# Four graph networks on one core: in the plain nodes' stream, the second and third layer's work moved one turn back

## The reference

```python
# network 0, four attention layers; a node always has itself as a neighbour
h = x @ W
alpha = leaky_relu((h @ a_s)[src] + (h @ a_d)[dst] + (ea @ We) @ a_e)
out = segment_sum(h[src] * segment_softmax(alpha, dst)[:, None], dst) + b
x = layernorm(out) * g + beta
# network 1: relations, three cells; messages relu(h[src] + relvec[rel])
# network 2: three layers
h = relu(h @ Ws0.T + mean_of_neighbours(h) @ Wn0.T + b0); prev = h
h = relu(h @ Ws1.T + mean_of_neighbours(h) @ Wn1.T + b1 + prev)
h = h @ Ws2.T + mean_of_neighbours(h) @ Wn2.T + b2
# network 3: products along edges, then a last layer norm
```

## Time and profile before

| what | value |
|---|---|
| time, median of 3 runs | 5097.33 us (5092.68 to 5098.29) |
| profiled execution | 5105.29 us, its span 5103.5 us |
| PE busy over the span | 3761.0 us, 74% |
| DVE busy | 3758.0 us, 74% |
| ACT busy | 3214.3 us, 63% |
| POOL busy | 2811.2 us, 55% |
| DMA, mean over the span | 210 GB/s |
| pass p1 | from 1237 to 1512 us of the span |
| pass p2 | from 1708 on, p3 from 2185 on |

### The profile page before, as it was taken

One profiled execution on the slowest core, in us unless ns is written; L12 is line 12 of the kernel. 1 busy time (PEld: TensorE's weight loads), 2 busy tenths in 40 slices (PEclk: granted clock), 3 DMA queues, 4 the chain that ended last, 5 costly groups with the idle time before them and its releaser, 6 DMA issues. The chain is left out here.

```text
span 5103.5 us, 104447 instructions
## 1 busy us (share of the span) xinstructions
PE 3761.0 (74%) x23663; PEld 3105.7 (61%) x23663; DVE 3758.0 (74%) x10843; ACT 3214.3 (63%) x11475; POOL 2811.2 (55%) x2759
## 2 busy tenths in 40 slices
PE   6365889966877677768776878788687887967775
PEld 5254778855557555645674655466576776856664
DVE  1576789978869786978796868699576775746666
ACT  2022779966868686968674533278586785646554
POOL 0474767702750473067104767676564765757776
PEclk9699999988998898989776767699899998978777
DMA  8899999955975696579664446567697996762221
GB/s 177 111 290 282 363 370 312 279 146 158 287 255 148 194 285 212 161 229 291 187 183 137 152 149 206 168 215 240 211 304 254 302 305 214 246 153 59 65 66 55
DMA packets 918273, 1074.23 MB, mean 210 GB/s; under 512 B 202779, under 2 KB 565065, under 8 KB 917106
## 3 DMA queue, kind: packets, MB, share of 16 engines
q1 hardware_dynamic: 763570, 890.24, 53.5%
q0 software_dynamic: 90944, 180.06, 14.4%
q10 hardware_dynamic: 63556, 1.81, 1.8%
HBM read 509.54 MB, written 566.14 MB: 211 GB/s over the span
## 5 line engine op out<-in xcount | busy, mean ns | idle before, releaser
L2366 POOL DMA_INDIRECT H<-gat_rows,src_i x784 | 802.4, 1023 | 870.0 <-POOLq L80 631.9
L1917 POOL DMA_INDIRECT s_G<-sage_rows,src_i x588 | 603.1, 1026 | 353.7 <-issue 162.5
L1696 POOL DMA_INDIRECT r_G<-rel_rows,idx x392 | 404.8, 1033 | 166.5 <-issue 117.4
L2555 PE MATMUL p_M<-Wg,p_hT 128*128 128x132 f32 x2352 | 340.3, 289 | 61.1 <-DVE p_res L2612 47.2
L2555 PEld LDWEIGHTS p_M<-Wg,p_hT 128*128 128x128 f32 x2352 | 294.8, 194 | 108.1 <-issue 91.7
L2612 DVE SCALAR_TENSOR_TENSOR p_res<-p_M,p_rr,cg 128x132 f32<-128x132 f32 x1176 | 333.8, 346 | 2.8 <-PE p_M L2555 1.9
L1709 PE MATMUL r_t<-r_oh,relv 8*128 8x512 f32 x294 | 205.3, 784 | 171.2 <-DMA r_G<-rel_rows,idx 72.8
L1305 PE MATMUL d_S<-ones,d_sqT 128*128 128x1 f32 x1568 | 226.1, 265 | 138.6 <-DVE d_ve L1450 138.5
L2694 PEld LDWEIGHTS p_pl_p<-Wn,p_pl_h 128*128 128x128 f32 x1568 | 202.3, 195 | 206.5 <-ACT p_pl_h L2788 159.6
L2694 PE MATMUL p_pl_p<-Wn,p_pl_h 128*128 128x128 f32 x1568 | 221.2, 286 | 137.4 <-ACT p_pl_h L2788 137.3
L1305 PEld LDWEIGHTS d_S<-ones,d_sqT 128*128 128x128 f32 x1568 | 219.5, 216 | 165.9 <-issue 128.3
(11 more groups left out here) (483 smaller groups left out, 12421.8 us busy)
## 6 DMA issues: line engine op xcount, KB each, us to landing
gat_rows<-p_res SPq DMA_DIRECT2D x294, 264.0 KB
sage_rows<-p_pl_s SPq DMA_DIRECT2D x294, 256.0 KB
gat_rows<-x_row SPq DMA_DIRECT2D x98, 536.0 KB
gat_rows<-d_res SPq DMA_DIRECT2D x147, 264.0 KB
d_hs<-gat_rows SPq DMA_DIRECT2D x147, 256.0 KB
s_hT<-sage_slots_t SPq DMA_DIRECT2D x147, 256.0 KB
slot_rows<-H SPq DMA_DIRECT2D x49, 544.0 KB
x_x<-in_x SPq DMA_DIRECT2D x98, 256.0 KB
```

Source lines behind the costliest of these rows:

```text
L1696: pool.indirect_dma_start(self.G[:, g % 4, k, :], None, table, bass.IndirectOffsetOnAxis(index[:, c:c + 1], 0), bounds_check=bound, oob_is ...
L1917: pool.indirect_dma_start(self.G[:, g % 4, k, :], None, kn.st[self.l], bass.IndirectOffsetOnAxis(kn.idx[:, c:c + 1], 0), bounds_check=boun ...
L2366: pool.indirect_dma_start(kn.H[:, c, 0:width], None, table, bass.IndirectOffsetOnAxis(index[:, c:c + 1], 0), bounds_check=bound, oob_is_er ...
L2555: mm = pe.matmul(self.pM[self.bank(b, j)][:, k // 2, (k % 2) * TW:(k % 2 + 1) * TW], self.hT[l][:, b.s2, k * P:(k + 1) * P], kn.Wg[:, l, : ...
```

## The change

In all engines' lists of `Plain`, rows1, hidden2, keep_h2, keep_rows(1) and the store of rows 1 get a lag that is larger by one, as do last, rows2, keep_rows(2), keep_z, and the stores of rows 2 and of z. On PE, rows1 and hidden2 also move ahead of the transposes in the order of a turn. No instruction is added or taken away; one turn more is needed until the last block is through.

```diff
-        steps = [(load, -2), (load_x, -1), (store_rows(0), 5), (store_rows(2), 6), (store_rows(1), 5), (store_z, 7), (store_n0, 2)]
+        steps = [(load, -2), (load_x, -1), (store_rows(0), 5), (store_rows(2), 7), (store_rows(1), 6), (store_z, 8), (store_n0, 2)]
...
-        return [(s, lag + 2, self.n) for s, lag in ((last, 6), (rows2, 6), (turn, 4), (rows1, 5), (hidden2, 5), (rows0, 4), (hidden1, 4))]
+        return [(s, lag + 2, self.n) for s, lag in ((last, 7), (rows2, 7), (rows1, 6), (hidden2, 6), (turn, 4), (rows0, 4), (hidden1, 4))]
...
-        steps = [(keep_h1, 5), (keep_rows(0, self.p0), 5), (keep_rows(2, self.p2), 6), (keep_n1, 4), (deviation_u, 3),
-                 (keep_h2, 5), (keep_rows(1, self.p1), 5), (square3, 0), (norm, 2), (deviation2, 1), (deviation3, 0), (square_u, 2)]
+        steps = [(keep_h1, 5), (keep_rows(0, self.p0), 5), (keep_rows(2, self.p2), 7), (keep_n1, 4), (deviation_u, 3),
+                 (keep_h2, 6), (keep_rows(1, self.p1), 6), (square3, 0), (norm, 2), (deviation2, 1), (deviation3, 0), (square_u, 2)]
...
-        steps = [(scale2, 2), (scale3, 1), (sums_u, 3), (keep_z, 6), (shift, 2), (gamma, 1), (scale_u, 3),
+        steps = [(scale2, 2), (scale3, 1), (sums_u, 3), (keep_z, 7), (shift, 2), (gamma, 1), (scale_u, 3),
```

## The result

| | before | after |
|---|---|---|
| median of 15 runs each, us | 5097.33 | 5085.99 |
| lowest to highest, us | 5090.76 to 5109.45 | 5075.05 to 5097.68 |
| profiled execution, us | 5105.29 | 5087.08 |
| its span, us | 5103.5 | 5085.3 |

The ratio is 0.9976, with a 95% interval of 0.9968 to 0.9985: the kernel became faster by 0.24%, a little more than the 0.2% that the prediction took as the edge.

What follows compares the result with a forecast made beforehand. The prediction took DVE's ring through one ACT instruction to bound the quiet turn, with barriers making each pass count. Terms 0 - 6 - 5 + 15 + 0 = +4 on 5097.3 gave 5101 us, range 5088 to 5113.

Steps and rivals of the forecast that it cites:

- quiet turns: Undisturbed 7.29 us turns: ACT's 0.46 us at keep_h2 go but come back at the square; 0 us.
- waits for z: DVE's keep_z waiting for store z to land: store issued 0.46 us earlier; -6 us, bounds 0 and -12.4.
- late hidden2 in mid-pass: PE delays in mid-pass now hit keep_n1 and deviation_u instead of add_shared; 0 us, 3 either way.
- ramp: Start of each pass, PE at half clock: first second-layer stall falls away or partly returns; -5 us, bounds -8 and -2.
- drain: End of each pass: one turn more, 5.0 us each; +15 us in all, bounds 13.2 and 17.6.
- So the quiet turn is DVE's, by way of one ACT instruction: Undisturbed turn: a DVE ring through ACT's square of add_shared's result sets 7.29 us, and the change touches none of it.
- The DMA engines would have to stand idle: Store z: issued earlier, it lands earlier only if DMA engines would else idle; none seen just before issue.
- They bound nothing: GpSimd's 196 gathers in the first pass: 201 us, over 12 us before the next stage begins, so no bound.
- rival (B): Faster: z waits -12.4, ramp -8, PE keeping its clock better -3, drain +13.2; -10, 5087 us, chance 0.13.
- (A): Drain alone counts: DMA engines keep the z waits, ramp stall returns a turn later; +13, 5110 us, chance 0.13.
- (C): keep_n1 becomes late as transposes behind two more groups miss ACT's turn; +15 in mid-pass, above 5116 us, chance 0.06.
- (D): Nothing but a shift, drain as cheap as the ramp is dear; 5097 us, chance 0.68 together with the forecast.

Runs made afterwards that it cites:

- e4: Changed kernel with the store of z moved ahead of the stores of rows 2 and 1 in SP's list; 5062.2 us, ratio 0.9958 to the kernel before.
- e6: Kernel before with square3 ahead of keep_h2 on ACT and the store of z at the head of SP's turn; 5061.1 us, ratio 0.9941.
- e7: Changed kernel's lags with PE's old order, and the store of z at the head of SP's turn; 5071.9 us, ratio 0.9961 to the kernel before.
- e3: Kernel before with only the store of z moved to the head of SP's turn; 5062.3 us, ratio 0.9949.
- e2: Kernel before with only ACT's list edited, square3 ahead of keep_h2; 5072.1 us, ratio 0.9969.
- e9: Kernel before with only the third layer (last, rows2, keep_rows(2), keep_z, stores of rows 2 and z) one turn later; 5107.0 us, ratio 1.0023.
- e8: Kernel before with the store of z first and half the edge-row gathers left out in the three passes (output incomplete); 5062.4 us, ratio 0.9943.
- e1: Changed kernel with PE's old order, transposes ahead of rows1 and hidden2, lags kept as changed; 5070.9 us, ratio 0.997 to the kernel before.

## Why the prediction was right or wrong, point by point

The forecast was +4 us; the passes gave -6.9. Term by term, by the means of two profiles each:

| term | forecast | measured |
|---|---|---|
| quiet turns | 0 | -4.5 |
| waits for z | -6 | -8.9 |
| late hidden2 in mid-pass | 0 | -3.6 |
| ramp | -5 | -6.7 |
| drain, with the two turns ahead of it | +15 | +16.7 |

**Quiet turns, 0: wrong, and this is the step that failed.** "So the quiet turn is DVE's, by way of one ACT instruction" took rows without a bracket for a chain without a delay. DVE alone could have made a turn in 7.21 us; ACT's round (its work, its 0.46 us of waiting at `keep_h2`, and the detour over `add_shared`) took 7.29, and the end of the norm released `add_shared`. The prediction said that ACT would merely get the 0.46 us back. It got back all but 0.08. In mid-pass this shows as 4.5 us less in DVE's records; e4, e6 and e7 against e3, where nothing waits for z, say 4.4 to 4.6. It is less than 74 times 0.08, and not every turn had the 0.08: eight of e3's 74 take 7.23 us. That ACT's wait was the cause is shown by e2 (wait covered, 7.21) against e3 and e9 (wait left, 7.29).

**Waits for z, -6: within its bounds, half as much again as forecast, and the reason not confirmed.** They fell by 8.9 us (from 15.4 to 6.5, means of two). The reason given, that store z goes out 0.46 us earlier, isn't needed. In the median it went out 4.28 us after `sums_u` before and 3.66 after the change, but also at 4.28 in e2, whose z waits are 8.6. What e2 and the change have in common is that the store of the norm, and with it the loads behind it in SP's queue, go out 0.5 to 0.6 us earlier. Whether that is the link wasn't tried. "The DMA engines would have to stand idle" as the condition for a gain fell with e3: their share rose, and all waits were gone.

The landing time of 3.0, 3.6 and 6.4 us in the earlier trace rows, from which the prediction took that z stands behind other packets, is not that of stores of z. The view counts all transfers that touch `plain_z_t`, and it holds landings only of loads in a later stage:

```profile
L2910 SPq DMA_DIRECT2D s_pe_zT<-plain_z_t x98: 327/354/433, 3606.5 to 4216.1; - x98
```

A store's landing can be read where `keep_z` waited for it: in p1's drain after the change (rows below) `keep_z` starts 1492.20 - 1488.55 = 3.65 us behind the issue of the store, and at the very end 1507.70 - 1505.29 = 2.41. In a quiet turn before, `keep_z` leaves the store about 7.29 - 4.28 + 0.60 = 3.6 us, so about a third of the stores came late; e3 leaves 8.7 us, and none did. Both are estimates from the marks of the timelines.

**Ramp, -5: right.** -6.7 us. The stall at the first full turn, 1.88 us of DVE in p1, came back at the transposes, as foreseen, in part:

```profile
1277.94 0.60 ACT L2775 ACTIVATE p_pl_nT<-p_pl_p_t 128x512 f32<-128x512 f32 x1 [0.88 <-PE p_pl_p_t L2701]
...
1278.76 0.18 DVE L2861 RECIPROCAL p_pl_rru<-p_pl_sdu 128x4 f32<-128x4 f32 x1 [0.92 <-ACT p_pl_sdu L2770]
```

0.92 us in p1; the interval in question is 7.93 us there and 7.32 and 6.56 in p2 and p3. In the second profile only p3 has such a stall, of 1.00 us. By windows, the granted clock after was 0.50 up to 1276 and 0.84 in 1275 to 1280, where it was 1.00 before:

```profile
1270.00:1276.00 6.00, 4.96 (x17) 3.93 (x18) 5.24 (x21) 4.44 (x13) 4.78 (x5) 0.50 0.59 169
1275.00:1280.00 5.00, 4.31 (x23) 3.33 (x22) 3.50 (x12) 3.82 (x9) 3.90 (x4) 0.84 0.86 245
```

Counted from a pass's first transfer, the ramp's last stretch at 1.2 GHz ended after 32.6 to 37.8 us in the six passes before and after 37.9 to 41.0 in the six after the change. This agrees in direction with what the page "TensorE: Matmul & The Clock Gate" of the Trainium skill (section "What's actually happening") states, that the half rate is the default and activity releases it. But in e2 and e3, whose second layer stays where it was, it ended after 39.6 to 40.4 us as well, so it isn't shown that thinner turns are the reason. And the stall did not come back in full, as the prediction worked out by that rule: it came in three passes of six, with 0.7 to 1.0 us, where five of six had had 1.9 to 2.2 before, and the ramp gave 6.7 us and not 2. e2, e3 and e9, in which the second layer stays where it was, have ramps of 108.2 to 110.3: the gain comes from the lags.

**Drain, +15: right in mechanism, a little small.** From the last `n1` (L2865) to the next stage the three passes took 19.55, 19.47 and 19.21 us before and 24.76, 25.47 and 24.69 after: +5.2, +6.0, +5.5, 16.7 in all, within the bounds of 13.2 and 17.6; the second profiles, where p1 ran into its gathers, say 19.0. The timeline of p1's end after:

```profile
1487.33 0.69 DVE L2865 TENSOR_TENSOR p_pl_u<-p_pl_u,p_pl_rru 128x512 f32<-128x512 f32 x1
...
1488.55 0.43 SPq L2680 DMA_DIRECT2D plain_z_t<-p_pl_zT  x1
...
1491.45 1.02 PE L2722 MATMUL p_pl_p_h<-p_pl_h,Ws 128*128 128x512 f32 x2
1492.20 0.75 DVE L2870 SCALAR_TENSOR_TENSOR p_pl_zT<-p_pl_p_z,sage_b,p_pl_nT 128x512 f32<-128x512 f32 x1 [4.18 <-DMA plain_z_t<-p_pl_zT]
...
1492.95 0.60 ACT L2775 ACTIVATE p_pl_nT<-p_pl_p_t 128x512 f32<-128x512 f32 x1 [1.59 <-DVE p_pl_zT L2870]
...
1498.10 1.02 PE L2722 MATMUL p_pl_p_h<-p_pl_h,Ws 128*128 128x512 f32 x2
1498.25 0.75 DVE L2870 SCALAR_TENSOR_TENSOR p_pl_zT<-p_pl_p_z,sage_b,p_pl_nT 128x512 f32<-128x512 f32 x1 [5.29 <-DMA plain_z_t<-p_pl_zT]
...
1502.65 1.02 PE L2722 MATMUL p_pl_p_h<-p_pl_h,Ws 128*128 128x512 f32 x2
1503.16 0.75 DVE L2870 SCALAR_TENSOR_TENSOR p_pl_zT<-p_pl_p_z,sage_b,p_pl_nT 128x512 f32<-128x512 f32 x1 [4.16 <-DMA plain_z_t<-p_pl_zT]
...
1505.29 0.43 SPq L2680 DMA_DIRECT2D plain_z_t<-p_pl_zT  x1
...
1507.70 0.75 DVE L2870 SCALAR_TENSOR_TENSOR p_pl_zT<-p_pl_p_z,sage_b,p_pl_nT 128x512 f32<-128x512 f32 x1 [3.79 <-DMA plain_z_t<-p_pl_zT]
...
1512.09 0.33 SPq L1168 DMA_DIRECT2D same_run<-same_as_before  x1
```

Four `keep_z` come after the last n1, one more than before, and each waits for the store of the last but one. The terms of the sum can be seen: hidden2 (L2722) of the last two blocks start 4.55 us apart, the added turn, for which 4.4 was taken, and from the last one to the next stage it takes 9.44 us, as the 9.45 before. In the table the drain grew by 18.9 and the two turns ahead of it shrank by 2.2, by the means of two profiles 16.7 as well. "They bound nothing" on the gathers was true by only 2 us: before, p1 ended 13.8 us after its last gather, against a floor of 11.8. The second profile of the change came close to it (13.0, with a drain of 30.41 us in p1), and e8 shows that it is the gathers.

**Late hidden2 in mid-pass, 0: too small.** DVE's waits for a late ACT at `add_shared` and `sums3`, 6.4 us, went away, and 2.8 us came at L2861: -3.6, just outside the 3 us that were kept either way. The traces point to the clock. In mid-pass of before TensorE falls to 0.50, which is 1.2 GHz, for a few microseconds at a time: six times in one profile and seven in the other; after, five times and two. One of them before and one after:

```profile
1319.00:1322.00 3.00, 3.00 (x11) 2.38 (x10) 2.75 (x11) 1.86 (x5) 2.12 (x3) 0.50 1.03 332
```

```profile
1376.00:1380.00 4.00, 4.00 (x13) 2.48 (x13) 3.68 (x14) 3.27 (x9) 3.06 (x4) 0.63 0.89 305
```

The second one in the timeline of the changed kernel, a turn further on:

```profile
1382.96 0.60 ACT L2775 ACTIVATE p_pl_nT<-p_pl_p_t 128x512 f32<-128x512 f32 x1 [0.99 <-PE p_pl_p_t L2701]
...
1383.77 0.18 DVE L2861 RECIPROCAL p_pl_rru<-p_pl_sdu 128x4 f32<-128x4 f32 x1 [0.86 <-ACT p_pl_sdu L2770]
```

Each of these 20 falls is followed by such a wait of DVE within 9 us, and there is none without a fall. A fall cost DVE about 0.95 us before (6.2 and 6.6 us for six and seven, at `add_shared` and `sums3`), and 0.5 to 0.9 after (at L2861). So the price of one was sized about right, and what came otherwise was their number. Each began 7 to 10 us behind a wait of DVE for z, and PE had stood idle for 1.8 to 3.8 us at a stretch just ahead of it, where the median of its long idle times (over 1 us) is 1.3 to 1.4 us. In e3, e4, e6, e7 and e8, which have no such waits, mid-pass holds no fall at all. So half of rival (B) took place: fewer waits for z, fewer falls. These are counts in twelve traces; no run moved the clock alone.

**Rivals.** (A) fell with e3. (B) named 5087 us, and 5086.0 was measured, but that it fits is luck: its drain of 13.2, its ramp of -8 and its 12.4 us of z waits did not come, and the turn of 7.21 us, which it doesn't have, did; only its 3 us for the clock are near what was found. (C) took place in seven mid-pass turns of the six passes profiled, each behind a fall of the clock, and not in quiet turns; that PE's order has a price is what e1 says. (D) was wrong in the same step as the forecast.

**What stays open.** The passes became 6.9 us shorter, the timed medians say 11.3 and 9.2. Over all kernels here the passes and the timed differences agree within 6 us, which is as far as the two methods reach; where the 2 to 4 us lie isn't known. Nor is the reason why e2 and the change have fewer waits for z, the largest term of mid-pass.

## What to carry to other kernels

Where two engines form a ring and are nearly level, work out each engine's own round (its busy time plus its waits) and compare them to a hundredth of a microsecond: the pace is set by the longer one, and what gives it away can be a delay of 0.06 us that no view lists, here worth 4.5 us in three passes. Before an instruction that waits is moved a whole turn back, which costs one turn more of draining in each pass (5 to 6 us here), look for ready work to put in front of it, and look at what stands in front of a store in its queue: moving `square3` and store z within their turns gave 0.59% against the change's 0.2%, with a drain 4 us longer in all, not 19.

## What the runs showed that I had not expected

- A store issued 5.3 us earlier in its turn took away all of its waits while the DMA engines became busier, 0.93 to 0.95: a share near 1 doesn't say that a given transfer can't land earlier.
- TensorE's granted clock falls to 0.50 for a few microseconds in the middle of a pass in which PE is busy for 152 of 190 us, and no fall came in the kernels in which nothing waits for z: 6 and 7 in the passes before, none in e3, where PE is busy for 156 of 190 us.
- From the last gather of GpSimd to the next stage behind the barrier at least 11.8 us go by, much more than the 4.4 us behind SP's last store when the gathers were over early.
